# Reordering the full rounds of the last stage of an attention and feed-forward kernel

## The chip, the cores and the metric

The kernel runs on 1 core of one Trainium2 chip. The metric is device time in microseconds (us), from one execution to the next the median of several runs. Engines are named as in the profile: PE (TensorE, matrix products), DVE (VectorE), ACT (ScalarE), POOL (GpSimd), SP (SyncE, which issues the DMAs).

## What is computed

A gated cross-attention, then a gated feed-forward layer, on x of 4 x 512 rows of 512. With `ln` the layer normalisation without weights, `act_quant` a rounding to 8-bit integers with one scale for each row, and the weights w1, w2 rounded to -1, 0, 1:

```
x = x + tanh(g_xattn) * (attention(ln(x), ctx) @ Wp + bp)      16 heads, 4096 keys
h = gelu(silu(act_quant(rms_norm(ln(x))) @ w1.T + b1))          2048 wide
h = (h - mean(h)) * rsqrt(var(h) + eps) * ln_g + ln_b
x = x + tanh(g_ffn) * (act_quant(rms_norm(h)) @ w2.T + b2)
```

## The kernel before

The queries, then the keys and values are projected; then `attend_and_finish` works through 256 units of attention (a head and a tile of 128 rows each). That takes until some 1535 us of the span. The last stage, which the change touches, follows: it takes the 16 tiles of 128 rows through the output projection and the feed-forward layer, two tiles (a pair) at a time, `PAIRS` = 8.

Each engine's program is written out by hand, in its own block, as a loop over rounds `r`. An engine executes its instructions strictly in that order, and semaphores (`wait_ge`, `after`) hold them until what they need is there. `pair_of(r)` gives the tiles (2r, 2r+1), or none outside 0 to 7. In round r four pairs are under way: `mixed` = pair r goes through the output projection, `fed` = pair r-1 through the first product, silu and gelu, `normed` = pair r-2 through the normalisation of the 2048 columns and its rounding, `done` = pair r-3 through the second product and the result. Rounds 3 to 7 hold all four: the full rounds. Rounds 1 and 2 lack `done`, rounds 8 to 10 lack `mixed` and drain the rest.

The steps, by engine (lines of the profile):

- PE: `turn_out(i)` transposes the attention's output of tile i (L1111, to `ps_v`); `project(i)` (L1121) multiplies it by Wp; `turn_ints(i)` transposes the rounded integers and their scales (L1167, L1168, to `ps_n`); `first_product(i)` is 16 matmuls L1181 and 4 matmuls L1182 in two halves of 1024 columns; `second_product(i)` is L1199 and 16 matmuls L1201.
- ACT: `keep_out(i)` copies what `turn_out` made (L1274); `centre(i)` (L1307) subtracts the row's mean; `silu(i)` (L1282) reads the first product's two halves; `gelu(i)` (L1287), `deviate(i)` (L1293, the sum of squared deviations), `square(i)` (L1302, the sum of squares after the normalisation), each over 2048 columns; `keep_ints(i)` (L1312, L1313) copies what `turn_ints` made, for the first product to read. Silu and Gelu need different activation tables: where one follows the other an ACT_TABLE_LOAD stands before it.
- DVE: `add_mixed(i)` (L1545, L1548, L1550) adds the projection to x and takes mean and variance; `largest`, `step_first`, `quantise_first` (L1554 to L1575) round tile by tile; `normalise(i)` is `centre_row` and `scale_row` (L1581, L1587); `largest_2` (L1595), `step_second` (L1603 to L1610) and `quantise_second` (L1622); `result(i)` (L1628).
- POOL: `negate_mean` (L1413), `scale_out` (L1408), `add_bias_2` (L1443), `invert_rms` (L1463, L1465), `mean` (L1447), `invert_sd`, `split_inverse`, `invert_dev` (L1451, L1453, for both tiles of a pair together).
- SP: loads of x, the transposes of the second integers, stores of the result.

Waits that matter here: `turn_ints(i)` waits for `keep_ints(i-1)`, since both tiles use the one `ps_n`:

```
after(pe, ints_kept, i)
```

`second_product(i)` waits for `result(i-1)`, since both use the one bank `ps_o` (up to tile 10). `project` of a pair's second tile waits for `add_mixed` of the first, for the same reason. `centre(i)` waits for `negate_mean(i)`, and this for `add_mixed(i)`.

Of the kernel before, what the change touches and what calls it, by code (L numbers as in the profile page):

```python
# [28 lines left out]
EPS = 1e-5  # L29
# [727 lines left out]
def attend_and_finish(nc, t, kept, o_sum, den, wp, bp, head_area, stored):  # L757


    with ExitStack() as stack:  # L760
# [216 lines left out]
        with nc.Block() as block:  # L977
# [100 lines left out]
            def _(pe):  # L1078
# [130 lines left out]
                for r in range(1, PAIRS + 3):  # L1209
                    mixed, fed, done = pair_of(r), pair_of(r - 1), pair_of(r - 3)  # L1210
                    for i in range(2):
                        if mixed:
                            turn_out(mixed[i])
                        if r == 1:
                            weigh(UNITS - 4 + 2 * i)
                        if fed:
                            first_product(fed[i])
                        if mixed:
                            project(mixed[i])
                        if r == 1:  # L1220
                            weigh(UNITS - 3 + 2 * i)
                    if r == 2:
                        sum_weights()
                    for i in done:
                        second_product(i)
                    for i in mixed:
                        turn_ints(i)

            @block.scalar
            def _(act):  # L1230
# [65 lines left out]
                def square(i):  # L1296
                    act.wait_ge(y_ready, i + 1)
                    if i % 2:
                        act.wait_ge(y_sq_ready, i)
                    elif i == 2 * LAST:  # L1300
                        act.wait_ge(dev_ready, QT)
# [40 lines left out]
                for r in range(1, PAIRS + 3):  # L1342
# [9 lines left out]
                    for i in normed:  # L1352
                        square(i)
                    if mixed:
                        keep_out(mixed[1])
                        centre(mixed[0])
                    if fed:
                        silu(fed[1])
                    if r == 1:
                        keep_heads(UNITS - 2)  # L1360
                    if r - 1 == LAST:
# [18 lines left out]
            def _(pool):  # L1380
# [68 lines left out]
                def invert_dev(r):  # L1449
                    pool.wait_ge(dev_ready, 2 * r + 2)  # L1450
                    pool.tensor_scalar(both(dev_mean, r), both(dev, r), 1.0 / INNER, EPS, ALU.mult, ALU.add).then_inc(dev_mean_ready, 1)  # L1451
                    pool.wait_ge(dev_mean_ready, r + 1)
                    pool.tensor_tensor(both(rstd_2, r), both(dev_mean, r), power[:, :], ALU.pow).then_inc(rstd_2_ready, 1)  # L1453

                def invert_dev_alone(i):
                    pool.wait_ge(dev_ready, i + 1)
                    pool.tensor_scalar(dev_mean[:, i:i + 1], dev[:, i:i + 1], 1.0 / INNER, EPS, ALU.mult, ALU.add).then_inc(dev_mean_ready, 1)
                    pool.wait_ge(dev_mean_ready, i - LAST + 1)
# [42 lines left out]
                for r in range(1, PAIRS + 2):  # L1501
# [14 lines left out]
                    for i in fed:  # L1516
                        mean(i)
                        if r - 1 == LAST:
                            invert_dev_alone(i)
# [282 lines left out]
```

## Time and profile before

| | us |
|---|---|
| median of 3 runs (lowest to highest) | 1773.95 (1773.41 to 1774.96) |
| the profiled execution's own time | 1778.12 |
| its span, first to last instruction | 1776.3 |
| busy in the span: PE, DVE, ACT, POOL | 1536.6, 1629.8, 1392.4, 1297.2 |
| mean granted clock of PE, share of full speed | 0.962 |

The span leaves 1.8 us of the profiled execution's time outside, and that execution took 4.2 us more than the median of the runs. A row of a timeline gives start, duration, engine, line and operation, what is written and read, and in brackets how long the engine was idle before it and what ended that; an interval between the starts of two rows is what the engine needs for what stands between them. In the windows view PEclk is the share of full clock granted to PE in that stretch.

### The profile page before, as it was taken

The page shows a single profiled execution, that of the slowest core. Times are in us where ns is not written, and L with a number is a line of the kernel's source. Part 1 is how long each engine was busy: PE and PEld are TensorE (multiplying, and loading weights), DVE is VectorE, ACT ScalarE, POOL GpSimd, SP SyncE. Part 2 cuts the span into 40 slices and gives each one's busy share as a digit, 9 for nine tenths or more (in the row PEclk, how much of TensorE's full clock was granted, in tenths as well). Part 3 has the DMA queues.
Part 4 walks back from the last instruction along what each step waited for, and adds up shares of the span by engine and source line. Part 5 has one row for each costly group of instructions (what it writes and reads, how often), then busy time and mean ns, then how long its engine had stood idle before and what let it go on. Part 6 is the DMA issues. An engine that isn't in the chain of part 4 may idle for free.

```text
span 1776.3 us, 34679 instructions
## 1 busy us (share of the span) xinstructions
PE 1536.6 (87%) x13207; PEld 753.7 (42%) x13207; DVE 1629.8 (92%) x2214; ACT 1392.4 (78%) x1351; POOL 1297.2 (73%) x1297
## 2 busy tenths in 40 slices
PE   7799967888888888988888998988888887789996
PEld 4344422444444444444444444444444443333332
DVE  7869968999999999999999999999999999378887
ACT  4468867788898878889888888987887786677874
POOL 0156755889889989888998998898998898453322
PEclk9989987999999999999999999999999998799998
DMA  6769976999968999995898998688988967214233
GB/s 207 256 201 357 329 259 126 169 174 172 164 125 139 169 177 179 171 169 107 148 183 166 183 178 156 114 144 161 151 158 135 152 136 146 65 36 95 53 73 83
DMA packets 725640, 282.62 MB, mean 159 GB/s; under 512 B 676121, under 2 KB 680793, under 8 KB 724194
## 3 DMA queue, kind: packets, MB, share of 16 engines
q1 hardware_dynamic: 724098, 277.47, 75.7%
q8 instruction: 105, 1.72, 0.4%
q0 software_dynamic: 704, 1.62, 0.3%
q10 hardware_dynamic: 672, 1.31, 0.2%
q14 instruction: 61, 0.50, 0.1%
HBM read 76.59 MB, written 35.95 MB: 63 GB/s over the span
## 4 chain that ended last, share of the span: by engine, by line
DVE 34%; POOL 21%; PE 14%; issue 11%; ACT 3%; DMA 2%; POOLq 0%; SPq 0%; DVEq 0%; ACTq 0%
DVE att_scaled L1663 32%; POOL att_probsT L1395 17%; PE att_scores L1181 4%; PE att_ps_o L1201 3%; PE att_scores L1121 2%; POOL att_low_row L1385 2%; PE att_scores L1141 2%; DMA att_pairsT<-att_pairs 2%; ACT att_pairs L1261 1%; POOL att_bias_row L1388 1%; PE att_scores L1182 1%; DVE att_v_largest L1632 1%; PE att_scores L1083 1%; PE att_ps_v L1111 1%; PE att_ps_v L1201 0%
## 5 line engine op out<-in xcount | busy, mean ns | idle before, releaser
L1663 DVE TENSOR_SCALAR_CACHE_REDUCE att_scaled<-att_scores,layer_nsq 128x1536 f32<-128x1536 f32 (+1 forms) x768 | 1202.2, 1639 | 19.6 <-PE att_scores L1141 14.6
L1261 ACT ACTIVATE att_pairs<-att_scaled,att_bias_row 128x4096 uint8<-128x4096 f32 x256 | 950.4, 3713 | 141.8 <-DMA att_pairsT<-att_pairs 92.1
L1395 POOL CAST att_probsT<-att_pairsT 128x2048 bf16<-128x2048 uint8 x512 | 953.6, 1891 | 107.7 <-DMA att_pairsT<-att_pairs 97.3
L1141 PE MATMUL att_scores<-first_head_area 96*128 96x512 bf16 x1024 | 297.8, 396 | 95.9 <-DVE att_scaled L1663 79.6
L1141 PE MATMUL att_scores<-att_head_area 96*128 96x512 bf16 x1024 | 289.7, 385 | 65.4 <-DVE att_scaled L1663 62.6
L1102 PEld LDWEIGHTS att_ps_o<-att_v_head,att_probsT 128*128 128x128 bf16 x8192 | 242.9, 96 | 65.3 <-issue 3.0
L1102 PE MATMUL att_ps_o<-att_v_head,att_probsT 128*128 128x32 bf16 x8192 | 245.1, 177 | 2.8 <-DMA att_v_head<-layer_w2T 2.5
L1141 PEld LDWEIGHTS att_scores<-first_head_area 96*128 96x128 bf16 x1024 | 81.6, 99 | 257.0 <-DVE att_scaled L1663 174.9
L1141 PEld LDWEIGHTS att_scores<-att_head_area 96*128 96x128 bf16 x1024 | 80.0, 98 | 214.1 <-DVE att_scaled L1663 151.3
L1083 PE MATMUL att_scores<-att_head_area 96*128 96x512 bf16 x621 | 170.2, 384 | 0.0
L1083 PE MATMUL att_scores<-first_head_area 96*128 96x512 bf16 x570 | 158.4, 388 | 0.0
L572 PE MATMUL kv_ps_k<-kv_weights_wk,kv_inT 128*128 128x512 f32 x256 | 117.9, 605 | 0.8 <-ACT kv_inT L623 0.8
L1385 POOL TENSOR_SCALAR att_low_row<-att_low 128x1 f32<-128x1 f32 x256 | 92.1, 360 | 31.2 <-DVE att_scaled L1663 30.9
L1091 PE MATMUL att_ps_v<-layer_w2T,layer_wp 128*128 128x512 f32 x192 | 99.9, 602 | 4.4 <-ACT layer_w1T L1235 4.3
L1252 ACT COPY layer_o_sum<-att_ps_o 128x32 f32<-128x32 f32 x256 | 43.8, 171 | 63.8 <-PE att_ps_o L1102 63.6
L1083 PEld LDWEIGHTS att_scores<-att_head_area 96*128 96x128 bf16 x621 | 61.1, 98 | 75.0 <-issue 2.7
L1083 PEld LDWEIGHTS att_scores<-first_head_area 96*128 96x128 bf16 x570 | 56.6, 99 | 70.8 <-issue 5.8
L1181 PE MATMUL att_scores<-layer_w1T,att_ints 128*128 128x512 bf16 x256 | 69.3, 395 | 0.1
L572 PEld LDWEIGHTS kv_ps_k<-kv_weights_wk,kv_inT 128*128 128x128 f32 x256 | 47.3, 195 | 49.2 <-issue 48.0
L1663 DVE DVE_READ_ACCUMULATOR att_scaled<-att_scores,layer_nsq 128x1 f32 x768 | 66.7, 87 | 0.0
L1388 POOL TENSOR_SCALAR att_bias_row<-att_low_row 128x1 f32<-128x1 f32 x256 | 48.7, 190 | 22.4
L682 POOL TENSOR_TENSOR kv_parts<-kv_rest,kv_parts 128x512 bf16<-128x512 f32 x32 | 41.4, 1293 | 24.7 <-ACT kv_parts L642 24.7
(181 smaller groups left out, 1599.8 us busy)
## 6 DMA issues: line engine op xcount, KB each, us to landing
layer_w2T<-ctx_T SPq DMA_DIRECT2D x96, 256.0 KB, 3.8
k_rows<-kv_parts SPq DMA_DIRECT2D x32, 392.0 KB, 4.1
q_w_in<-in_L_ffn_w_dram SPq DMA_DIRECT2D x32, 256.0 KB, 2.8
kv_weights_ctx_in<-in_ctx_dram SPq DMA_DIRECT2D x32, 256.0 KB, 4.8
kv_weights_w_in<-in_L_ffn_w_dram SPq DMA_DIRECT2D x32, 256.0 KB, 4.9
ctx_T<-kv_inT SPq DMA_DIRECT2D x8, 1024.0 KB, 6.6
q_x_in<-in_x_dram SPq DMA_DIRECT2D x16, 256.0 KB, 3.7
terns<-kv_tern SPq DMA_DIRECT2D x32, 128.0 KB, 4.5
```

The source lines that it names most:

```text
L572: last = pe.matmul(ps_k[n % 2][:, :], turned[:, k, at:at + P], wk[:, k, :], start=(k == 0), stop=(k == CT - 1))
L1083: pe.matmul(spare, q_head[slot][:, at:at + P], k_head[slot][:, 0:C], start=True, stop=True)
L1091: pe.matmul(ps_v[:, :], wp[:, k, group * P:(group + 1) * P], ctx_chunk[n % RING], start=(k == 0), stop=(k == CT - 1)).then_inc(chunk_done, 1)
L1102: last = pe.matmul(ps_o[:, 0:D], probsT[r % C_BUFS][:, k, :], v_head[h % 2][:, k * D:(k + 1) * D], start=(k == 0), stop=(k == KT - 1))
L1141: last = pe.matmul(buffer[:, x:x + 512], q_head[slot][:, at:at + P], k_head[slot][:, STARTS[j] + x:STARTS[j] + x + 512], start=True, stop= ...
L1181: pe.matmul(bank, ints_1[i % 2][:, k, :], kept["w1T"][:, k, j:j + C], start=(k == 0), stop=False)
L1201: last = pe.matmul(bank[:, :], turned[i % TURN_BUFS][:, k, :], kept["w2T"][:, k, :], start=False, stop=(k == IT - 1))
L1261: act.activation(pairs[g % R_BUFS][:, :].bitcast(U8).rearrange("p (c two) -> p two c", two=2), scaled[u][:, :].rearrange("p (two c) -> p t ...
L1385: pool.tensor_scalar(low_row[:, :], low[u][:, 0:1], low[u][:, 1:2], low[u][:, 2:3], ALU.min, ALU.min).then_inc(low_ready, 1)
L1388: pool.tensor_scalar(bias_row[:, u:u + 1], low_row[:, :], 1.0, LOG255, ALU.mult, ALU.add).then_inc(row_ready, 1)
L1395: pool.tensor_copy(probsT[g % C_BUFS][:, parity * HALF:(parity + 1) * HALF, :].rearrange("p k q -> p (k q)"), bytes_now.rearrange("p (n tw ...
L1663: dve.tensor_scalar(scaled[u][:, STARTS[j]:STARTS[j] + WIDTHS[j]], scores[(g * NCH + j) % 2][:, 0:WIDTHS[j]], kept["nsq"][:, g:g + 1], Non ...
```

## The change

In the full rounds (r = 3 to 7) the order of the work is another on three engines, and a few neighbouring steps follow.

- PE: the round was turn_out, first_product, project for each tile, then both second products, then both turn_ints. Now: first product of tile one, project of tile one, turn_out of tile two, second product of tile one, project of tile two, first product of tile two, second product of tile two. In all rounds up to 6, `turn_out` of the next round's first tile stands between the two `turn_ints`.
- ACT, full rounds: gelu and deviate of tile one come before the centring of the second mixed tile, silu and gelu of tile two behind it, then both `keep_ints`, and last `deviate` of tile two.
- POOL: `invert_dev` is done tile by tile in all rounds; in full rounds tile one's comes right after its `mean`, tile two's `mean` and `invert_dev` last.
- DVE: `result` of tile one stands before `largest` of tile one instead of behind it.

```diff
--- before.py
+++ after.py
@@ -1208,23 +1208,35 @@
 
                 for r in range(1, PAIRS + 3):
                     mixed, fed, done = pair_of(r), pair_of(r - 1), pair_of(r - 3)
-                    for i in range(2):
-                        if mixed:
-                            turn_out(mixed[i])
-                        if r == 1:
-                            weigh(UNITS - 4 + 2 * i)
-                        if fed:
-                            first_product(fed[i])
-                        if mixed:
-                            project(mixed[i])
-                        if r == 1:
-                            weigh(UNITS - 3 + 2 * i)
-                    if r == 2:
-                        sum_weights()
-                    for i in done:
-                        second_product(i)
-                    for i in mixed:
-                        turn_ints(i)
+                    if mixed and done:
+                        first_product(fed[0])
+                        project(mixed[0])
+                        turn_out(mixed[1])
+                        second_product(done[0])
+                        project(mixed[1])
+                        first_product(fed[1])
+                        second_product(done[1])
+                    else:
+                        for i in range(2):
+                            if mixed and (i or r == 1):
+                                turn_out(mixed[i])
+                            if r == 1:
+                                weigh(UNITS - 4 + 2 * i)
+                            if fed:
+                                first_product(fed[i])
+                            if mixed:
+                                project(mixed[i])
+                            if r == 1:
+                                weigh(UNITS - 3 + 2 * i)
+                        if r == 2:
+                            sum_weights()
+                        for i in done:
+                            second_product(i)
+                    if mixed:
+                        turn_ints(mixed[0])
+                        if r + 1 < PAIRS:
+                            turn_out(2 * r + 2)
+                        turn_ints(mixed[1])
 
             @block.scalar
             def _(act):
@@ -1297,8 +1309,8 @@
                     act.wait_ge(y_ready, i + 1)
                     if i % 2:
                         act.wait_ge(y_sq_ready, i)
-                    elif i == 2 * LAST:
-                        act.wait_ge(dev_ready, QT)
+                    else:
+                        act.wait_ge(dev_ready, i + 2)
                     act.activation(squares, rows[i % ROW_BUFS], ACT.Square, accum_out=y_sq[:, i:i + 1]).then_inc(y_sq_ready, 1)
 
                 def centre(i):
@@ -1351,13 +1363,24 @@
                         keep_heads(UNITS - 3)
                     for i in normed:
                         square(i)
+                    late = bool(mixed and pair_of(r - 3))
                     if mixed:
                         keep_out(mixed[1])
                         centre(mixed[0])
-                    if fed:
+                    if fed and not late:
                         silu(fed[1])
                     if r == 1:
                         keep_heads(UNITS - 2)
+                    if late:
+                        gelu(fed[0])
+                        deviate(fed[0])
+                        centre(mixed[1])
+                        silu(fed[1])
+                        gelu(fed[1])
+                        keep_ints(mixed[0])
+                        keep_ints(mixed[1])
+                        deviate(fed[1])
+                        continue
                     if r - 1 == LAST:
                         for i in fed:
                             gelu(i)
@@ -1446,16 +1469,10 @@
                     pool.wait_ge(gelu_ready, i + 1)
                     pool.tensor_tensor(mean_neg[:, i:i + 1], h_sum[:, i:i + 1], inv_n[:, :], ALU.mult).then_inc(mean_ready, 1)
 
-                def invert_dev(r):
-                    pool.wait_ge(dev_ready, 2 * r + 2)
-                    pool.tensor_scalar(both(dev_mean, r), both(dev, r), 1.0 / INNER, EPS, ALU.mult, ALU.add).then_inc(dev_mean_ready, 1)
-                    pool.wait_ge(dev_mean_ready, r + 1)
-                    pool.tensor_tensor(both(rstd_2, r), both(dev_mean, r), power[:, :], ALU.pow).then_inc(rstd_2_ready, 1)
-
-                def invert_dev_alone(i):
+                def invert_dev(i):
                     pool.wait_ge(dev_ready, i + 1)
                     pool.tensor_scalar(dev_mean[:, i:i + 1], dev[:, i:i + 1], 1.0 / INNER, EPS, ALU.mult, ALU.add).then_inc(dev_mean_ready, 1)
-                    pool.wait_ge(dev_mean_ready, i - LAST + 1)
+                    pool.wait_ge(dev_mean_ready, i + 1)
                     pool.tensor_tensor(rstd_2[:, i:i + 1], dev_mean[:, i:i + 1], power[:, 0:1], ALU.pow).then_inc(rstd_2_ready, 1)
 
                 def invert_rms(r):
@@ -1513,18 +1530,23 @@
                             invert_rms_alone(i)
                     elif normed:
                         invert_rms(r - 2)
-                    for i in fed:
+                    late = bool(mixed and pair_of(r - 3))
+                    for i in fed[:1] if late else fed:
                         mean(i)
-                        if r - 1 == LAST:
-                            invert_dev_alone(i)
+                        if late or r - 1 == LAST:
+                            invert_dev(i)
                     if mixed:
                         negate_mean(mixed[1])
                         invert_sd(r)
                         if r + 1 < PAIRS:
                             scale_out(2 * r + 3)
                         split_inverse(r)
-                    if fed and r - 1 != LAST:
-                        invert_dev(r - 1)
+                    if late:
+                        mean(fed[1])
+                        invert_dev(fed[1])
+                    elif r - 1 != LAST:
+                        for i in fed:
+                            invert_dev(i)
                     if r == 1:
                         pool.wait_ge(pv_ready, UNITS)
                         pool.memset(sum_parts, 0.0).then_inc(fin_const, 1)
@@ -1582,7 +1604,7 @@
 
                 def scale_row(i):
                     row = rows[i % ROW_BUFS]
-                    dve.wait_ge(rstd_2_ready, i // 2 + 1 if i < 2 * LAST else i - LAST + 1)
+                    dve.wait_ge(rstd_2_ready, i + 1)
                     dve.wait_ge(u_ready, i + 1)
                     dve.scalar_tensor_tensor(row, row, rstd_2[:, i:i + 1], ln_b, ALU.mult, ALU.add).then_inc(y_ready, 1)
 
@@ -1685,10 +1707,10 @@
                         quantise_second(i)
                     if mixed:
                         add_mixed(mixed[1])
-                        largest(mixed[0])
                     if done:
                         result(done[0])
                     if mixed:
+                        largest(mixed[0])
                         largest(mixed[1])
                         step_first(r)
                         for i in mixed:
```

On ACT, from gelu of tile one to the end of the round, in a full round (`att_ints_0` and `att_ints_1` are keep_ints of the two tiles, `att_v_head` the centring of the second). Before:

```order
L1287 ACT_TABLE_LOAD
L1287 ACTIVATE att_scaled,att_h_sum<-att_scaled 128x2048 x2
L1293 ACTIVATE att_head_area,att_dev<-att_scaled,att_mean_neg 128x2048
L1307 ACTIVATE att_v_head<-layer_o_sum,att_mean_less 128x512
L1293 ACTIVATE att_head_area,att_dev<-att_scaled,att_mean_neg 128x2048
L1312 ACTIVATE att_ints_0<-att_scores 128x512
```

Now (the lines are those of the changed file):

```order
L1299 ACT_TABLE_LOAD
L1299 ACTIVATE att_scaled,att_h_sum<-att_scaled 128x2048
L1305 ACTIVATE att_head_area,att_dev<-att_scaled,att_mean_neg 128x2048
L1319 ACTIVATE att_v_head<-layer_o_sum,att_mean_less 128x512
L1294 ACT_TABLE_LOAD
L1294 ACTIVATE att_scaled<-att_scores,att_step 128x1024 x2
L1299 ACT_TABLE_LOAD
L1299 ACTIVATE att_scaled,att_h_sum<-att_scaled 128x2048
L1324 ACTIVATE att_ints_0<-att_scores 128x512
L1325 COPY att_inv_T<-att_scores 9x128
L1324 ACTIVATE att_ints_1<-att_scores 128x512
```

Silu of tile two (`att_scores,att_step`) moved from before the first table load to behind the centring, and brought two more table loads with it; a full round has four instead of two.

On PE, the end of a round, `+` is the change (L1167 and L1168 are turn_ints, L1111 is turn_out):

```order
 L1167 MATMUL att_scores<-layer_ident,layer_bp 128x128 x4
 L1168 MATMUL att_scores<-layer_identb,att_inv_parts 9x128
+L1111 MATMUL att_ps_v<-layer_ident,first_head_area 128x128 x4
 L1167 MATMUL att_scores<-layer_ident,layer_bp 128x128 x4
 L1168 MATMUL att_scores<-layer_identb,att_inv_parts 9x128
-L1111 MATMUL att_ps_v<-layer_ident,first_head_area 128x128 x4
```

The transposes of the next tile's output moved from behind the second turn_ints to between the two. SP's order is the same in both kernels.

## Rows read from the trace of the kernel before

**Rows 1.** Windows view, one full round; us, busy of PE, PEld, DVE, ACT, POOL, PEclk.
```profile
1607.00:1636.10 29.10, 27.18 (x109) 10.90 (x108) 24.52 (x31) 22.53 (x26) 9.09 (x20) 1.00 0.33 73
```

**Rows 2.** Waits view, PE, 1607.1 to 1723.4 us; total, times, longest.
```profile
PE att_ps_o L1199 <- DVE layer_o_sum L1628: 4.0, 4, 1.0
```

**Rows 3.** Timeline of PE, round 4 and the start of the next.
```profile
1636.18 0.38 PE L1167 MATMUL att_scores<-layer_ident,layer_bp 128*128 128x128 f16 x4
...
1637.62 0.38 PE L1167 MATMUL att_scores<-layer_ident,layer_bp 128*128 128x128 f16 x4 [0.91 <-ACT att_inv_T L1313]
...
1638.09 0.66 PE L1111 MATMUL att_ps_v<-layer_ident,first_head_area 128*128 128x128 f32 x4
1638.58 1.03 PE L1181 MATMUL att_scores<-layer_w1T,att_ints 128*128 128x512 bf16 x4
...
1643.71 3.70 PE L1121 MATMUL att_scores<-layer_wp,first_head_area 128*128 128x512 f32 x8
...
1665.24 0.38 PE L1167 MATMUL att_scores<-layer_ident,layer_bp 128*128 128x128 f16 x4
```

**Rows 4.** Timeline of PE, end of rounds 6 and 7.
```profile
1695.74 0.38 PE L1167 MATMUL att_scores<-layer_ident,layer_bp 128*128 128x128 f16 x4 [0.91 <-ACT att_inv_T L1313]
...
1725.17 0.38 PE L1167 MATMUL att_scores<-layer_ident,layer_bp 128*128 128x128 f16 x4 [0.91 <-ACT att_inv_T L1313]
```

**Rows 5.** Timeline of ACT, round 4.
```profile
1636.75 0.60 ACT L1312 ACTIVATE att_ints<-att_scores 128x512 bf16<-128x512 f16 x1 [1.97 <-PE att_scores L1168]
...
1642.59 2.35 ACT L1282 ACTIVATE att_scaled<-att_scores,att_step 128x1024 f32<-128x1024 f32 x2
1644.83 1.90 ACT L1302 ACTIVATE att_head_area<-att_scaled 128x2048 bf16<-128x2048 f32 x1
...
1649.53 0.72 ACT L1307 ACTIVATE first_head_area<-layer_o_sum,att_mean_less 128x512 f32<-128x512 f32 x1
...
1652.93 1.11 ACT L1282 ACTIVATE att_scaled<-att_scores,att_step 128x1024 f32<-128x1024 f32 x1 [1.40 <-PE att_scores L1182]
1654.06 1.28 ACT L1287 ACT_TABLE_LOAD   x1
1655.35 1.91 ACT L1287 ACTIVATE att_scaled<-att_scaled 128x2048 f32<-128x2048 f32 x1
...
1661.14 0.71 ACT L1307 ACTIVATE att_v_head<-layer_o_sum,att_mean_less 128x512 f32<-128x512 f32 x1
1661.76 1.99 ACT L1293 ACTIVATE att_head_area<-att_scaled,att_mean_neg 128x2048 bf16<-128x2048 f32 x1
```

**Rows 6.** Timeline of DVE, round 4.
```profile
1644.22 2.35 DVE L1587 SCALAR_TENSOR_TENSOR att_scaled<-att_scaled,att_rstd 128x2048 f32<-128x2048 f32 x1
1647.52 0.75 DVE L1545 SCALAR_TENSOR_TENSOR layer_o_sum<-att_scores,layer_gate_tanh,att_scaled 128x512 f32<-128x512 f32 x1 [0.95 <-PE att_scores L1121]
...
1649.03 0.18 DVE L1550 BATCH_NORM_AGGREGATE att_mv<-att_stats 128x2 f32<-128x6 f32 x1
...
1654.07 0.16 DVE L1603 TENSOR_TENSOR att_row<-att_y_max,att_rms 128x2 f32<-128x2 f32 x1 [0.49 <-POOL att_rms L1465]
...
1658.90 0.18 DVE L1550 BATCH_NORM_AGGREGATE att_mv<-att_stats 128x2 f32<-128x6 f32 x1
```

**Rows 7.** Timeline of PE, three idle times away from the full rounds.
```profile
294.21 1.01 PE L1102 MATMUL att_ps_o<-att_v_head,att_probsT 128*128 128x32 bf16 x32 [2.49 <-DMA att_v_head<-layer_w2T]
...
1495.79 0.76 PE L1141 MATMUL att_scores<-att_head_area 96*128 96x512 bf16 x2 [1.65 <-DVE att_scaled L1663]
...
1769.08 0.37 PE L1199 MATMUL att_ps_v<-att_probsT,att_less 64*128 64x512 bf16 x1 [1.86 <-issue]
```

**Rows 8.** Windows view, behind each of these; columns as in rows 1.
```profile
294.20:297.60 3.40, 3.39 (x39) 1.74 (x40) 1.29 (x2) 2.35 (x2) 1.93 (x2) 0.56 1.02 194
...
1495.80:1499.20 3.40, 3.40 (x9) 1.20 (x10) 2.87 (x4) 2.26 (x2) 2.69 (x5) 0.54 0.52 98
...
1769.00:1773.00 4.00, 3.92 (x17) 1.58 (x17) 0.00 (x0) 0.00 (x0) 0.00 (x0) 1.00 0.35 134
```

## The prediction

> **What bounds the kernel now.** I read the windows view first. In a full round PE is busy 27.18 of 29.10 us, ACT 22.53, DVE 24.52 [rows 1]: the last stage hangs on PE, at full clock. The waits view then says what keeps PE from being busy throughout: in four rounds it waits 4.0 us for `result`, before the second of two second products (1.00 each) [rows 2], and in each round 0.91 for `keep_ints`, between the two `turn_ints` [rows 3]. The chain of waits runs through PE alone in these rounds, with those two detours. A round, from `turn_ints` to `turn_ints`, is 1665.24 - 1636.18 = 29.06 us [rows 3]; the last one, between second `turn_ints`, 1725.17 - 1695.74 = 29.43 [rows 4]. Work and issue on PE are 29.06 - 1.00 - 0.91 = 27.15.
>
> **What the change aims at.** It puts project, first product and a second product between things that waited for each other, so the 1.00 goes. Before `result` is waited for again, PE has a project (3.70) and a first product (5.13 = 1643.71 - 1638.58 [rows 3]) to do. `turn_out`, 0.49 us (1638.58 - 1638.09 [rows 3]), moves into the 0.91. PE alone would then need 27.15 + 0.91 - 0.49 = 27.57 a round. The question is what is late next.
>
> **ACT is.** Before, silu and gelu of tile two were finished when the centring of the second mixed tile ran at 1661.14; behind it stood one `deviate`, and ACT was then idle 1.97 before `keep_ints` [rows 5]. Now load, silu, load and gelu stand between the centring and `keep_ints`, and PE's second `turn_ints` waits for `keep_ints`. The next first product and project follow on PE, then `add_mixed` on DVE, and from there the next centring: a loop through three engines, once a round. Its length, step by step:
>
> - `add_mixed` of tile one to `step_second`, through POOL's part as before: 1654.07 - 1647.52 = 6.55 [rows 6].
> - `step_second` to the end of tile two's mean and variance: 1658.90 + 0.18 - 1654.07 = 5.01 [rows 6].
> - From there over POOL to a centring on ACT: 1649.53 - 1649.21 = 0.32 [rows 5, 6]. ACT has nothing left before it by then; `deviate` of tile one is done.
> - Centring, 0.62 (1661.76 - 1661.14); table load 1.29 (1655.35 - 1654.06); silu, two halves, 2.24 (1644.83 - 1642.59); table load 1.29; gelu 1.91 [rows 5]. Sum 7.35. Both halves of the first product are there by then.
> - `keep_ints` to the second `turn_ints`: 1637.62 - 1636.75 = 0.87 [rows 3, 5].
> - `turn_ints` 0.47, first product 5.13, project to `add_mixed` 1647.52 - 1643.71 = 3.81 [rows 3, 6].
>
> Together 29.51 us, against 29.06 now. The loop, not PE, sets the round, and PE idles 29.51 - 27.15 = 2.36 us in one piece, at the second `turn_ints`, where it had 1.00 and 0.91 apart. The two added loads are 2.58 of the 29.51; without them PE would bound.
>
> **The sum without the clock.** I count from second `turn_ints` to second `turn_ints`. The end of round 2: `turn_out` is already done, the next first product starts 0.49 earlier, so -0.49. Rounds 3 to 6: 4 x (29.51 - 29.06) = +1.80. Round 7: 29.51 - 29.43 = +0.08. The drain behind it (rounds 8 to 10) starts with a first product straight after that `turn_ints` in both kernels and is PE's, then DVE's chain as before: 0. In all +1.4 us. A latency that I took 0.1 wrong at two or three of the six hand-overs makes 0.3 a round, so this term lies between 0 and +3.
>
> **Other edits, at nothing.** `deviate` of tile two, now last, starts once the second `keep_ints` is through (0.57 us after the second `turn_ints`, 0.6 long) and takes 1.99 [rows 5], so it ends 3.2 us after it, which is 6.5 after the first `turn_ints` (0.47 + 0.49 + 2.36 = 3.32 lie between the two); normalising that row takes DVE two operations of 2.35 [rows 6], so to 11.2, while the projection that DVE needs next ends at 3.32 + 0.47 + 5.13 + 3.70 = 12.6. The cover is 1.4 us; DVE idles longer, nothing more. The loads of the silu table at the round's start stood in an idle time of ACT and still do. ACT's total rises by 2.58 to some 25, under 29. POOL is busy 9.09 of 29.10 [rows 1]; inverting tile by tile adds under 1 us to that, and its `mean` and inversion for tile one end while the centring's mean is not yet there. `result` moved by one step: its wait falls away because PE now ends that product much earlier. SP's queue is unchanged; the transposes of the second integers have a whole round before they are used.
>
> **A rule that speaks against the change.** After silu's last half (start 1652.93, 1.11 long, end 1654.04) the load starts at 1654.06, and gelu at 1655.35, 0.01 after the load's end [rows 5]: a switch costs 1.29 and nothing beside it. The Trainium skill (ScalarE: Activation LUTs, section "What ACT_TABLE_LOAD costs") states about 1283 ns for the load, which the trace confirms, and a drain of about 1380 ns with it, 2.66 us a switch, which the trace doesn't show here. By the page the two switches in the loop would be 5.3 instead of 2.6. Its advice, in the section "Rules for kernel authors", is to do all of one table set before switching; the change does the opposite.
>
> **The clock.** This is the largest unknown, since no full round of before has an idle time of 2.36. The nearest rows: PE idle 2.49 and, elsewhere, 1.65 us; behind both the granted clock fell to its lower level, 1.2 GHz, and averaged 0.56 and 0.54 over the next 3.40 us [rows 7, 8]. One such stretch costs 3.40 x 0.46 = 1.6 us of PE's work, and PE's work behind the stall lies in the loop, so nobody takes it up. Against it stands one idle time of 1.86 in the drain, with the clock at 1.00 over the next 4 us [rows 7, 8], and the full rounds themselves, where 1.00 and 0.91 left the clock at 1.00 [rows 1]. There are five stalls (ends of rounds 3 to 7). The bounds are 0 and 5 x 1.6 = 8.0 us. 2.36 is nearest to 2.49, which fell, but in our stall dense products stand close on both sides, as in the one that didn't: I take three of five, 4.8 us.
>
> **Forecast.** +1.4 + 4.8 = +6.2 us. Against the profiled execution's 1778.12 this is 1784.3; that one lay 4.2 above the median, so for the median 1773.95 + 6.2 = 1780.2.
>
> **Rivals.**
>
> 1. *The clock holds* through all stalls or all but one: 1775.4 to 1777.0. For it: the idle time of 1.86. Against it: two of the three rows. That is within 0.2% of before (3.5 us, about what a measurement of this kernel can tell from no change).
> 2. *PE bounds, and the change is faster.* If ACT reaches `keep_ints` 29.51 - 27.57 = 1.94 us earlier in the round than I sum, the stall is gone and every round takes 27.57: 0.49 + 4 x 1.49 + 1.86 = 8.3 us less, 1765.6. The place is the pair of table loads behind the centring; hidden, they give 2.58. For it: each engine's busy time would fit. Against it: loads stand in the engine's order between the centring and what needs them, and the load in front of gelu in the rows started only after silu. Part of it (a loop shorter by 0.7) would give a time near 1772.
> 3. *A table switch drains ACT.* A load that holds the engine for longer than its own 1.28 us when activations stand on both sides, as it does in the loop, makes each round longer twice. The rows speak against it: 0.02 before and 0.01 behind. With 1 us more a load it would be 10 us in five rounds, 1785.4. The Trainium skill's figure (same page and section as above) would give 5 x 2 x 1.38 = 13.8 us, an estimate of 1789.2.
>
> **Chances.** Forecast, two to five low stretches, 1778.6 to 1783.4: 0.62. Clock holds: 0.25. PE bounds, or nearly: 0.10. Drain: 0.03. Slower by over 0.2% is then 0.65, within 0.2% 0.25, faster 0.10. The range goes from 1772, where a shorter loop begins, to 1785, five low stretches and a loop longer by 0.3: it leaves out most of rivals 2 and 3.
>
> **What would show it.** In the profile after: four table loads in each full round; ACT idle before the centring of the second tile and not before `keep_ints`; PE without a wait for `result`, with one of 2.4 us for `keep_ints`; rounds of 29.5, and of 31 where the clock fell. Rounds of 27.6 with a wait of 0.4 would prove rival 2, rounds of 31.5 or more at full clock rival 3. I would be wrong altogether if ACT waited for PE at the end of a round.

## The result

The change makes the kernel slower: 1792.8 us median of 4 runs (1787.71 to 1793.27) against 1773.68 of before, a ratio of 1.0097 with the 95% interval 1.0085 to 1.011 (the two medians alone divide to 1.0108). Forecast were 1780.2 us and a range that ended at 1785: the direction was right, the size was not. The profiled execution took 1793.27 us, span 1791.5, mean granted clock 0.954 (before 0.962).

All of it lies in the last stage. Counted in the profiled execution of each kernel, this stage runs from the second `turn_ints` of round 1 (before 1546.94, after 1543.15) to the end of the span (1776.3, 1791.5): 229.4 us before, 248.4 after, 19.0 more. Everything ahead of it is the same work, and ended 3.8 us earlier in this execution.

The windows view of the changed kernel, from each second `turn_ints` to the next (PE, PEld, DVE, ACT, POOL busy, PEclk), answers to [rows 1]:

```profile
1605.30:1638.90 33.60, 31.02 (x108) 11.52 (x108) 24.43 (x32) 25.21 (x28) 12.88 (x21) 0.86 0.27 63
1638.90:1672.80 33.90, 31.25 (x108) 11.60 (x109) 24.77 (x32) 25.21 (x28) 12.88 (x21) 0.85 0.27 62
1672.80:1705.30 32.50, 29.87 (x109) 11.51 (x110) 24.79 (x32) 25.21 (x28) 12.88 (x21) 0.90 0.25 58
1705.30:1737.50 32.20, 29.41 (x105) 10.97 (x106) 24.02 (x31) 25.21 (x28) 11.24 (x19) 0.89 0.23 50
```

Before, a round was 29.06 us with the clock at 1.00. Now the four are 33.6, 33.9, 32.5 and 32.2, and the clock averages 0.85 to 0.90. ACT is 2.7 us busier, with two more table loads of 1.28 us. PE is busy 2 to 4 us more with the same instructions: the time is in slower matmuls.

The waits view, 1605 to 1740 us, answers to [rows 2]:

```profile
PE att_scores L1167 <- ACT att_inv_T L1325: 13.3, 5, 2.8
...
ACT att_v_head L1319 <- POOL att_mean_less L1436: 12.3, 4, 3.1
```

No wait for `result` is left. Five waits for `keep_ints` (the ends of rounds 3 to 7) take 13.3 us, 2.6 to 2.8 each. ACT waits 3.1 us a round ahead of the centring of the second tile. Both are as the prediction described them.

The timeline of PE at the end of round 5, the counterpart of [rows 3]:

```profile
1669.07 0.38 PE L1167 MATMUL att_scores<-layer_ident,layer_bp 128*128 128x128 f16 x4
...
1669.54 0.66 PE L1111 MATMUL att_ps_v<-layer_ident,first_head_area 128*128 128x128 f32 x4
1672.81 0.59 PE L1167 MATMUL att_scores<-layer_ident,layer_bp 128*128 128x128 f16 x4 [2.62 <-ACT att_inv_T L1325]
...
1673.53 1.89 PE L1181 MATMUL att_scores<-layer_w1T,att_ints 128*128 128x512 bf16 x4
...
1675.89 1.89 PE L1181 MATMUL att_scores<-layer_w1T,att_ints 128*128 128x512 bf16 x4
...
1678.24 1.52 PE L1181 MATMUL att_scores<-layer_w1T,att_ints 128*128 128x512 bf16 x4
...
1680.01 1.04 PE L1181 MATMUL att_scores<-layer_w1T,att_ints 128*128 128x512 bf16 x4
...
1681.30 3.70 PE L1121 MATMUL att_scores<-layer_wp,first_head_area 128*128 128x512 f32 x8
```

Four matmuls of L1181 take 1.89 us in the first two groups, then 1.52, then 1.04, about the 1.03 of before. From 1672.81 to the start of the project is 8.49 us; before, those steps were 0.47 and 5.13, together 5.60.

ACT's timeline ahead of it, the counterpart of [rows 5]:

```profile
1664.58 0.72 ACT L1319 ACTIVATE att_v_head<-layer_o_sum,att_mean_less 128x512 f32<-128x512 f32 x1 [3.07 <-POOL att_mean_less L1436]
1665.32 1.28 ACT L1294 ACT_TABLE_LOAD   x1
1666.61 2.12 ACT L1294 ACTIVATE att_scaled<-att_scores,att_step 128x1024 f32<-128x1024 f32 x2
1668.75 1.28 ACT L1299 ACT_TABLE_LOAD   x1
1670.05 1.91 ACT L1299 ACTIVATE att_scaled<-att_scaled 128x2048 f32<-128x2048 f32 x1
...
1671.95 0.58 ACT L1324 ACTIVATE att_ints<-att_scores 128x512 bf16<-128x512 f16 x1
```

Centring, load, silu, load, gelu, then `keep_ints`, without a gap: 7.37 us from 1664.58 to 1671.95, where the prediction had summed 7.35. Two loads of 1.28 stand in it, each followed by its activation within 0.01 to 0.02 us.

### The profile page after: what moved, and what is told of

Same layout as the page of the kernel before. It is cut to its first block, busy times and chain, and to the rows that moved or that the text cites. A ratio compares the mean times of both kernels' runs of the same rounds, so it can differ in the third digit from the quotient of the medians.

```text
span 1791.5 us, 34710 instructions
## 1 busy us (share of the span) xinstructions
PE 1552.0 (87%) x13207; PEld 755.9 (42%) x13207; DVE 1629.2 (91%) x2214; ACT 1406.1 (78%) x1361; POOL 1324.3 (74%) x1311
## 4 chain that ended last, share of the span: by engine, by line
DVE 43%; POOL 16%; issue 11%; PE 8%; ACT 4%; DMA 2%; POOLq 0%; SPq 0%; DVEq 0%; ACTq 0%
DVE att_scaled L1685 40%; POOL att_probsT L1418 11%; PE att_scores L1141 2%; DMA att_pairsT<-att_pairs 2%; PE att_scores L1181 2%; ACT att_pairs L1273 1%; POOL att_low_row L1408 1%; POOL layer_o_sum L1466 1%; POOL att_bias_row L1411 1%; DVE att_v_largest L1654 1%; ACT att_scaled L1294 1%; PE att_scores L1083 1%; PE att_scores L1121 1%; PE att_scores L1182 1%; ACT att_head_area L1305 1%
## 5 line engine op out<-in xcount | busy, mean ns | idle before, releaser
L1181 PE MATMUL att_scores<-layer_w1T,att_ints 128*128 128x512 bf16 x256 | 82.5, 455 | 0.0
L1685 DVE DVE_READ_ACCUMULATOR att_scaled<-att_scores,layer_nsq 128x1 f32 x768 | 63.0, 82 | 0.0
```

Source lines behind the costliest of these rows:

```text
L1181: pe.matmul(bank, ints_1[i % 2][:, k, :], kept["w1T"][:, k, j:j + C], start=(k == 0), stop=False)
L1685: dve.tensor_scalar(scaled[u][:, STARTS[j]:STARTS[j] + WIDTHS[j]], scores[(g * NCH + j) % 2][:, 0:WIDTHS[j]], kept["nsq"][:, g:g + 1], Non ...
```

## The experiments

Two theories. A: the loop through PE, DVE and ACT is as long as summed, and what makes the rounds long is the lower clock behind the stall. B: the loop itself is longer, because the last deviation is late and holds DVE. The changed kernel can't tell them apart, since the slow matmuls are in the loop as well.

**e1: the stall filled.**

```diff
+ def keep_warm(times):
+     for _ in range(times):
+         pe.matmul(mixed_bank(2), kept["w1T"][:, 0, 0:P], kept["w1T"][:, 0, 0:C], start=True, stop=True)
...
                              turn_out(2 * r + 2)
+                         if done:
+                             keep_warm(11)
                          turn_ints(mixed[1])
```

> The change with 11 spare matmuls of 512 columns (some 2.4 us) put on TensorE ahead of the second turn_ints of each full round, into a PSUM area that is free then; nothing else differs. Theory A (the lower clock behind the stall took most of the 19 us): the stall is filled, the clock stays at 1.00 in all full rounds, a round is the loop at full clock, 29.7 to 29.9 us, and the kernel takes 1776 to 1778. Theory B (the loop itself is longer than summed, through the late deviation and VectorE held up, whatever the clock): rounds stay above 31 us and the kernel above 1784.

Measured: 1775.16 us median against 1774.19 of before in the same runs, ratio 1.0003 (0.9989 to 1.0018). Windows and timeline of PE:

```profile
1633.20:1662.80 29.60, 29.33 (x120) 12.06 (x121) 24.77 (x32) 24.99 (x28) 12.86 (x21) 1.00 0.31 72
```

```profile
1633.24 0.38 PE L1167 MATMUL att_scores<-layer_ident,layer_bp 128*128 128x128 f16 x4 [0.24 <-ACT att_inv_T L1331]
...
1662.79 0.38 PE L1167 MATMUL att_scores<-layer_ident,layer_bp 128*128 128x128 f16 x4 [0.24 <-ACT att_inv_T L1331]
```

The clock is at 1.00 in all four rounds, and a round is 1662.79 - 1633.24 = 29.55 us; both this and the time lie a little below what was expected. The loop had been summed at 29.51. Theory A holds and B falls: with spare work in the stall the change costs nothing that can be measured. The clock then took 1792.8 - 1775.2 = 17.6 us. Round by round, against e1's interval of the same round: 4.1 and 4.3 us behind the first two stalls (33.66 and 33.87 against 29.55), 2.9 and 3.1 behind the next two, 2.8 in the drain; 17.2 in all, 3.4 for a stall on the mean.

**e2: no table switch.**

```diff
- ACT.Silu,
+ ACT.Gelu,
```

The first activation of the feed-forward layer is thus another function, and the values of the layer are others; the run is for its time alone. All four table loads of a full round are gone with it, not only the two that the change added.

> The change with Gelu in the place of Silu, so that no table switch is left in the last stage; the values of the feed-forward layer are therefore others. Theory A (two table loads behind the centring put ScalarE into the path by 1.9 us, the stall then costs the clock): without them ScalarE reaches keep_ints before TensorE does, no stall over 0.5 us, clock 1.00, rounds of 27.6, the kernel at 1764 to 1767. Rival (the order of ScalarE's work, not the loads, holds TensorE up): the stall stays over 1.5 us, the clock falls, 1780 or more.

Measured: 1760.83 us, ratio 0.9923 (0.99 to 0.9946). Timeline of PE, full rounds 4 and 5:

```profile
1627.21 0.38 PE L1167 MATMUL att_scores<-layer_ident,layer_bp 128*128 128x128 f16 x4 [0.33 <-ACT att_inv_T L1325]
...
1654.48 0.38 PE L1167 MATMUL att_scores<-layer_ident,layer_bp 128*128 128x128 f16 x4 [0.33 <-ACT att_inv_T L1325]
```

The stall is 0.33 us and the round 27.27: PE bounds. So it is the loads that come with ACT's new order, not the order by itself, that bring ACT into the path. That it is the two behind the centring is read from the loop, in which only these two stand; the run took out all four. The time is below the range expected; the loads of rounds 1, 2 and 8 go too, which the expectation left out (TensorE's idle time at the end of round 1 is 8.65 us, in the change 10.07).

**e3: a part of the change alone.** `turn_out` of the next pair between the two `turn_ints`, all else as before.

```diff
-                         if mixed:
+                         if mixed and (i or r == 1):
                              turn_out(mixed[i])
...
-                     for i in mixed:
-                         turn_ints(i)
+                     if mixed:
+                         turn_ints(mixed[0])
+                         if r + 1 < PAIRS:
+                             turn_out(2 * r + 2)
+                         turn_ints(mixed[1])
```

> The kernel before with one part of the change alone: turn_out of the next pair's first tile between the two turn_ints. Theory: 0.49 us of the 0.91 wait is covered in each round, rounds of 28.6, in all 7 x 0.45 to 0.49: 1770.3 to 1771. Rival (the wait for the integers just grows elsewhere, VectorE or ScalarE sets the round): 1773 to 1774.

Measured: 1770.82 us, ratio 0.998 (0.9968 to 0.9992).

```profile
1632.01 0.38 PE L1167 MATMUL att_scores<-layer_ident,layer_bp 128*128 128x128 f16 x4 [0.33 <-ACT att_inv_T L1316]
...
1655.31 0.37 PE L1199 MATMUL att_ps_o<-att_probsT,att_less 64*128 64x512 bf16 x1 [1.00 <-DVE layer_o_sum L1631]
...
1660.59 0.38 PE L1167 MATMUL att_scores<-layer_ident,layer_bp 128*128 128x128 f16 x4 [0.33 <-ACT att_inv_T L1316]
```

A round is 28.58 us, 0.48 less than before; the wait for `keep_ints` shrank from 0.91 to 0.33 and the 1.00 for `result` stayed. This part is worth 3.4 us between the medians; the interval holds 1.4 to 5.7.

**e9, e10: the other two halves.** e9 has TensorE's new program and the other engines' old ones; e10 the reverse.

> TensorE's new order alone, the other engines as before. Laid out from the rows of before: ScalarE does both gelus and the first deviation only after silu of the second tile, which now waits for a product that comes late in the round; the second centring and all behind it are late, TensorE waits over 8 us for the integers each full round, rounds of 36 us, 1773.7 + 4 x 7 to 5 x 7 + what the clock costs: 1802 to 1820. Rival (TensorE's order alone would have done and ScalarE's reordering is the mistake): under 1774.

> The new orders of ScalarE, GpSimd and VectorE, with TensorE's order as before. Laid out: keep_ints still comes behind load, silu, load, gelu, so a stall of 1.9 us before the second turn_ints stays and the wait of 1.0 us for result as well; rounds of 30.0 at full clock, +5 us, and 1.6 to 4 us more for each fall of the clock behind the stall: 1779 to 1795. Rival (ScalarE's new order costs nothing by itself): 1773 to 1775.

Measured: e9 1817.61 us (2 runs), ratio 1.0241 (1.022 to 1.0261); e10 1780.7 us, ratio 1.0042 (1.0028 to 1.0055). Timelines of PE, e9 then e10:

```profile
1648.34 0.58 PE L1167 MATMUL att_scores<-layer_ident,layer_bp 128*128 128x128 f16 x4 [8.15 <-DVE layer_bp L1587]
...
1685.92 0.59 PE L1167 MATMUL att_scores<-layer_ident,layer_bp 128*128 128x128 f16 x4 [8.15 <-DVE layer_bp L1587]
```

```profile
1603.41 0.38 PE L1167 MATMUL att_scores<-layer_ident,layer_bp 128*128 128x128 f16 x4 [2.47 <-ACT att_inv_T L1313]
...
1633.44 0.38 PE L1167 MATMUL att_scores<-layer_ident,layer_bp 128*128 128x128 f16 x4 [1.93 <-ACT att_inv_T L1313]
```

With TensorE's order alone the wait for the integers is 8.15 us and a round 37.6 (laid out at full clock: 36.0; the clock falls behind such a wait as well), so ACT's silu of tile two had to move behind the centring if the first product was to come so late. With the others' orders alone a round is 30.03 us at full clock, as laid out, with stalls of 2.47, three times 1.9 and, in round 7, 1.22. Behind only one of them did the clock fall. The windows view of e10, behind the 2.47 and behind the wait of 1.95 that ended at 1693.49:

```profile
1603.40:1633.40 30.00, 27.09 (x108) 10.93 (x108) 23.98 (x32) 25.21 (x28) 13.56 (x22) 1.00 0.29 68
...
1693.40:1696.80 3.40, 3.31 (x14) 1.70 (x14) 3.25 (x2) 2.73 (x5) 0.94 (x1) 0.59 0.06 22
```

Each half is slower than before by itself.

**e5, e6, e8: how long may the stall be?** e1 with 5, 8 and 2 spare matmuls in the place of 11.

> As e1, with 5 spare matmuls (1.1 us) instead of 11: an unbroken idle time of some 1.5 us is left in each full round, between the two lengths that the rows of before bracket (1.00 held, 1.65 fell once). Theory A (the clock falls after some of the stalls, and what a fall costs here is 3 to 4 us): a time between e1 and the change, 1778 to 1788, with the granted clock at its lower level behind two to four of the five stalls. Rival (any filling of the stall keeps the clock): 1775 to 1777. Rival (only a stall under 1 us keeps it): as the change, 1788 to 1793.

> As e1 with 8 spare matmuls (1.7 us); some 0.9 us of idle time is left. Theory A: the clock holds as behind the 1.00 us wait of the kernel before, 1775 to 1777, as e1. Rival (the stall's length is not what decides, the transposes around it count too): one to three stalls still fall, 1779 to 1785.

> As e1 and e5 with only 2 spare matmuls (0.4 us): some 2.2 us of each stall are left. Theory (the longer the unbroken idle time, the longer the clock stays low behind it: none behind 0.9, 3.4 us behind two of five at 1.5, 6.8 to 10.2 us behind all five at 2.6): most of the five fall, some of them for only 3.4 us, rounds of 31 to 33, 1783 to 1790. Rival (the length of the low stretch has nothing to do with the idle time's): lengths as in the change, 1790 to 1793.

Measured, with e1 and the change beside them (ratios to before of their own runs):

| spare matmuls | idle left, us | of 5 stalls, clock fell behind | PE time lost by a fall, us | median us | ratio (95%) |
|---|---|---|---|---|---|
| 11 (e1) | 0.25 | 0 | | 1775.16 | 1.0003 (0.9989 to 1.0018) |
| 8 (e6) | 0.90 | 0 | | 1776.68 | 1.0016 (1.0003 to 1.003) |
| 5 (e5) | 1.54 | 2 | 1.4 to 1.6 | 1778.72 | 1.002 (1.0007 to 1.0032) |
| 2 (e8) | 2.19 | 3 | 2.9 to 3.1 | 1784.64 | 1.0079 (1.0047 to 1.0111) |
| 0 (the change) | 2.62 | 5 | 2.8 to 4.3 | 1792.8 | 1.0097 (1.0085 to 1.011) |

The middle columns are one profiled execution each. The time lost is the interval to the next second `turn_ints` less e1's: 1636.78 - 1605.63 = 31.15 in e5, 1665.53 - 1632.91 = 32.62 in e8, against 29.55; behind the fifth stall it is the drain, less e1's. e8's five executions reach from 1782.37 to 1797.33, on both sides of the change's four; the longest of them pulls its ratio above the 1.0063 of the two medians. So the times of e8 and of the change are not told apart. The windows view behind a stall, in steps of 3.4 us; e5, whose stall ended at 1605.63:

```profile
1605.60:1609.00 3.40, 3.37 (x14) 1.14 (x14) 1.82 (x2) 2.79 (x5) 0.00 (x0) 0.78 0.00 0
1609.00:1612.40 3.40, 3.40 (x11) 0.93 (x10) 2.68 (x2) 2.80 (x3) 2.90 (x2) 0.71 0.00 0
1612.40:1636.80 24.40, 22.87 (x91) 9.65 (x91) 20.04 (x30) 19.61 (x21) 9.97 (x19) 1.00 0.37 87
```

e8, whose second stall ended at 1632.91:

```profile
1632.90:1636.30 3.40, 3.39 (x11) 1.06 (x12) 1.99 (x1) 2.58 (x4) 0.00 (x0) 0.50 0.01 3
1636.30:1639.70 3.40, 3.40 (x9) 0.83 (x7) 2.49 (x2) 1.84 (x4) 2.90 (x2) 0.50 0.00 0
1639.70:1643.10 3.40, 3.40 (x12) 1.31 (x11) 2.21 (x1) 2.60 (x4) 0.00 (x0) 1.00 0.00 0
```

The change, whose stall ended at 1638.94:

```profile
1638.90:1642.30 3.40, 3.36 (x11) 1.09 (x12) 2.03 (x1) 2.54 (x3) 0.00 (x0) 0.50 0.01 2
1642.30:1645.70 3.40, 3.40 (x9) 0.83 (x7) 2.45 (x2) 1.84 (x4) 2.90 (x2) 0.50 0.00 0
1645.70:1649.20 3.50, 3.50 (x9) 0.92 (x8) 2.25 (x1) 1.45 (x3) 0.00 (x0) 0.59 0.00 0
```

Behind 1.54 us the time at the lower level is some 3.4 us (0.78 and 0.71 over two steps), behind 2.19 two steps of 0.50, behind 2.62 two steps and most of a third. So in this row of kernels the longer idle time costs more often and, from 1.54 to 2.19, more each time. PE is busy in every one of these steps: being busy does not bring the clock back at once. Nor does it always fall in the idle time itself: in e5 it fell some 1.9 us after the restart, with PE busy again. Where between 0.90 and 1.54 it begins to fall in this place was not tried.

The length of the idle time alone does not decide, though. In e10, above, the clock held behind 2.47 us, longer than the 2.19 behind which it fell three times of five. And e4, below, has one idle time of 4.08 us, at the end of round 2, with some 3.4 us at the lower level behind it, half as much as behind 2.19:

```profile
1570.81 0.38 PE L1169 MATMUL att_scores<-layer_ident,layer_bp 128*128 128x128 f16 x4 [4.08 <-DVE layer_bp L1579]
```

```profile
1571.20:1574.60 3.40, 3.40 (x14) 1.59 (x14) 3.26 (x3) 1.98 (x6) 3.18 (x3) 0.50 0.00 0
1574.60:1578.00 3.40, 3.40 (x14) 1.10 (x14) 3.40 (x2) 1.49 (x2) 3.32 (x3) 1.00 0.03 7
```

The kernels also differ in what TensorE does ahead of the wait: e10 has another wait, of 1.00 us, that ends 4.3 us ahead, and no `turn_out` between the two `turn_ints`; the 4.08 of e4 stand in a round without second products. What decides beside the length is not shown by any run here.

**e4, e7: versions that beat both.** e3, with the other wait removed in a way that keeps ACT's two gelus together: second products alternate between two banks, so none waits for the `result` just before it; ACT centres the second tile before the first deviation; DVE takes both results last (its lines are left out below, as are those of e3).

```diff
-             return ps_v if i >= APART and i % 2 else ps_o
+             return ps_v if i % 2 else ps_o
...
+                     if i % 2 == 0:
+                         after(pe, result_ready, i - 6)
...
+                     if i % 2:
+                         pe.wait_ge(out_kept, min(i + 7, QT))
+                     after(pe, result_ready, i - 1)
...
                          if mixed:
                              centre(mixed[1])
                          if fed:
                              deviate(fed[0])
```

> e3 with the other wait removed in another way than the change does: the second products alternate between two PSUM banks in all rounds, so the second one doesn't wait for result; ScalarE keeps its two gelus together and centres the second tile before the first deviation; VectorE takes both results last. Laid out from the rows of before, TensorE alone sets the round: 27.6 to 27.8 us, 1765 to 1767. Rival (a new wait of the same size, for the scales' split on GpSimd or for the centring): rounds of 28.5, 1770 to 1771.

Measured: 1764.04 us, ratio 0.9942 (0.992 to 0.9964).

```profile
1629.40:1657.20 27.80, 27.11 (x111) 10.92 (x109) 24.82 (x32) 22.75 (x26) 9.06 (x19) 1.00 0.32 76
1657.20:1685.00 27.80, 27.08 (x110) 10.89 (x109) 24.82 (x32) 22.75 (x26) 9.06 (x19) 1.00 0.32 77
```

A round is 27.8 us, of which PE is busy 27.1, at full clock and with two table loads. That is as laid out; the time is 1 us below the range. e7 adds 36 and 16 spare matmuls to e4 where TensorE idles at the ends of rounds 1 and 2.

> e4 with spare matmuls on TensorE, 36 and 16 of them, in the idle times at the ends of rounds 1 and 2 (8.95 and 4.08 us in e4), into a bank that is free then. Theory A (a fall of the clock behind an idle time costs 2 to 3 us of TensorE's work where that is in the path): both restarts run at full clock, 3 to 5 us less than e4, 1759 to 1761. Rival (TensorE's slow restart in these two rounds is hidden by VectorE and ScalarE): as e4, 1763 to 1765.

Measured: 1763.34 us, ratio 0.994 (0.992 to 0.9961). Timeline of PE in e7, the second `turn_ints` of round 2 and the first of round 3:

```profile
1570.18 0.38 PE L1169 MATMUL att_scores<-layer_ident,layer_bp 128*128 128x128 f16 x4 [0.33 <-ACT att_inv_T L1323]
...
1598.20 0.38 PE L1169 MATMUL att_scores<-layer_ident,layer_bp 128*128 128x128 f16 x4 [1.85 <-DVE layer_bp L1585]
```

The two restarts ran at full clock: each `turn_ints` took 0.38 us, where e4 has 0.59 for both of round 1 and 0.58 for the second of round 2. Between second `turn_ints`, round 2 then took 27.52 us against 29.60 in e4. But round 3 took 29.79 against 29.42, with TensorE idle for 1.85 us near its end instead of 0.79; behind that the clock fell (0.50 over 3.4 us), and round 4 took 28.77 against 27.75. Of the 2.1 us gained 1.4 were spent again, and the medians show the other 0.7, too little to be told from nothing. The rival holds: e7 can't be told from e4.

## Why the prediction was wrong, and where it was right

- **The loop.** Right, to a few hundredths: 29.51 summed, 29.55 in e1. So was its part on ACT (7.35 against 7.37). The idle time in it was 2.62 where 2.36 had been summed: TensorE's own work and issue in a round are 26.93, the 29.55 of e1 less the 2.62, not 27.15 (27.27 - 0.33 = 26.94 in e2).
- **The sum without the clock.** +1.4 forecast; e1 has +1.0 between medians and an interval that holds both that and zero. The total is right, partly by luck, for two of its terms are not. There are only three intervals of 29.06 us between second `turn_ints`, not four: the one from round 2 to round 3 was 30.62 us before. It is 31.97 in e1, so +1.35 where -0.49 stood; the loop holds there as well, with TensorE's matmuls at the lower clock at its start in both kernels. Against that, round 2 got 0.64 shorter, which the sum leaves out, and round 7 0.30 shorter instead of 0.08 longer. With 3 x 0.50 for the three rounds and 0.09 for the drain, the stage of e1 is 2.0 us longer in the profiled executions.
- **The edits at nothing.** The late deviation kept DVE waiting 1.60 us ahead of `centre_row` and 0.73 ahead of `scale_row`. DVE still waited 3.28 us for the projection behind it, but with PE at its lower clock. At full clock, in e1, 0.67 us of the cover of 1.4 are left: it held, by half of what was worked out. POOL's part was too low, 3.8 us more in a round (12.88 against 9.09) where under 1 had been put; the last section says where they are. They lengthened no round. Timeline of DVE, the change and e1:

```profile
1676.40 2.35 DVE L1603 SCALAR_TENSOR_TENSOR att_scaled<-att_scaled,att_mean_neg,att_head_area 128x2048 f32<-128x2048 f32 x1 [1.60 <-ACT att_head_area L1305]
1679.48 2.35 DVE L1609 SCALAR_TENSOR_TENSOR att_scaled<-att_scaled,att_rstd 128x2048 f32<-128x2048 f32 x1 [0.73 <-POOL att_rstd L1476]
1685.11 0.75 DVE L1567 SCALAR_TENSOR_TENSOR layer_o_sum<-att_scores,layer_gate_tanh,first_head_area 128x512 f32<-128x512 f32 x1 [3.28 <-PE att_scores L1121]
```

```profile
1642.66 0.75 DVE L1573 SCALAR_TENSOR_TENSOR layer_o_sum<-att_scores,layer_gate_tanh,att_scaled 128x512 f32<-128x512 f32 x1 [0.67 <-PE att_scores L1121]
```

- **The rule on table switches.** That a switch costs its load "and nothing beside it" stood: in the loop, between activations on both sides, each load took 1.28 us and no drain was seen, by the Trainium skill (ScalarE: Activation LUTs, "What ACT_TABLE_LOAD costs") 1.38 us more. Rival 3 fell. The Trainium skill's advice (same page, "Rules for kernel authors") to do all of one set before switching was right for this kernel, as far as e2 and e4 show it: e2, without any switch, and e4, with two a round, are both faster than the change with its four, though neither takes out the two extra switches alone.
- **The clock: the step that failed.** The prediction took three stalls of five, at 1.6 us: 4.8. Measured were five of five, at 2.8 to 4.3: 17.2. Both factors were low, the second by more. The 1.6 came from 3.4 us at 0.54 to 0.56 behind idle times of 1.65 and 2.49 in the attention [rows 7, 8], and I took that as the price of any fall. e5 shows that such a price is right for an idle time of 1.54 in this stage; for 2.2 to 2.6 in this place it is twice to nearly three times as much. Why a stretch lasted 3.4 us behind the 2.49 in the attention and 6.8 to 10.2, part of it still in the stall, behind 2.62 here stays open. The same stage had rows that warned of it: at the ends of rounds 1 and 2, behind idle times of 10.07 and 5.14 us, the matmuls ran at the lower clock for some 5 us after the restart (before, 1545.24 to 1550.7 and 1576.25 to 1581.4). The prediction does not use them. The upper bound of 8.0 us was five times the same low price, and that is why the range ended too early: an upper bound has to bound the price as well as the number.
- **The rivals.** "The clock holds" and "PE bounds" both fell in the change itself; e1 and e2 are the kernels in which they are true, at 1775.2 (forecast for the first 1775.4 to 1777.0) and 1760.8 (for the second 1765.6; e2 also lacks the other loads).

## What to carry to other kernels

Filling one engine's gaps by reordering is worth what the busy-time sums say only if the new order leaves every loop through the other engines shorter than the round; follow one full loop, with the table loads that the new neighbours cause. Two short waits are not the same as one long one on TensorE: 1.00 and 0.91 apart cost 1.9 us, 2.62 in one piece cost those 2.6 and on the mean 3.4 more (in e10, 2.47 cost nothing more). Where such a stall can't be avoided, spare matmuls in it can keep the clock up; here eleven a round were worth 17.6 us.

## What was not expected of the hardware

The time at the lower clock did not follow the length of the idle time: some 3.4 us behind 1.54 in e5 and behind 4.08 in e4, 6.8 behind 2.19, 6.8 to 10.2 behind 2.62, none behind 2.47 in e10. Where it came, it went on although PE was busy.

On POOL the 128x1 operation that scales the deviation took 0.19 us before for two tiles (0.29 once), and after as much as 2.35. Timeline of POOL in the change:

```profile
1661.59 1.12 POOL L1474 TENSOR_SCALAR att_dev_mean<-att_dev 128x1 f32<-128x1 f32 x1 [2.21 <-ACT att_head_area L1305]
...
1676.45 2.35 POOL L1474 TENSOR_SCALAR att_dev_mean<-att_dev 128x1 f32<-128x1 f32 x1 [4.06 <-ACT att_head_area L1305]
1678.89 0.56 POOL L1476 TENSOR_TENSOR att_rstd<-att_dev_mean,att_power 128x1 f32<-128x1 f32 x1
```

The one at 1676.45 ended at 1678.80, just after DVE's `centre_row` of 2.35 us that had started at 1676.40; the one at 1661.59 ended at 1662.71, just after DVE's two `quantise_second`, which ran from 1660.17 to 1662.65. All five full rounds show the same pair. So it ends with the DVE operation beside it; what holds it was not tried. It makes the late tile's inversion come some 2 us later, but `scale_row` waits only 0.73 us for that, since `centre_row` ran until 1678.75 in any case. In e1 this wait is 0.72, about as much as the cover of 1.4 lost.
